# Two layer norms, the linear layer and the set-up of the second attention, split by batch and placed inside the two attentions

## The reference

```python
x = x + _L0_attn_ref(_layernorm(x), ...)  # causal softmax attention, 16 heads of 64, then proj
x = x + _L0_ffn_ref(_layernorm(x), ...)   # base = x @ W.T plus a routed low-rank term, below
x = x + _L1_attn_ref(_layernorm(x), ...)  # softmax of minus squared distances, 16 heads of 8
x = x + _L1_ffn_ref(_layernorm(x), ...)   # shared expert + 2 of 8 experts of width 512
```

## Time and profile before

| | us |
|---|---|
| median of three runs | 1101.64 (1101.56 to 1103.21) |
| the profiled execution, whole | 1099.16 |
| its span, first to last instruction | 1097.4 |
| mean granted TensorE clock in the span | 0.961 |

### The profile page before, as it was taken

How to read it: one execution, slowest core, us unless ns; L and a number is a source line. 1 busy time by engine, 2 the same in 40 slices (tenths; PEclk the granted TensorE clock), 3 DMA queues, 4 the chain that set the end, 5 groups by cost and what they waited for, 6 DMA issues and landing times.

```text
span 1097.4 us, 18772 instructions
## 1 busy us (share of the span) xinstructions
PE 1004.7 (92%) x6927; PEld 596.8 (54%) x6927; DVE 700.0 (64%) x1454; ACT 707.4 (64%) x1031; POOL 556.2 (51%) x482
## 2 busy tenths in 40 slices
PE   4789999999999999999467999999998399999997
PEld 3456666666666666665353222233222277888786
DVE  6777777777777767773463223353122589999998
ACT  3356656666666656665224999999998376666564
POOL 2267877777787778778100000000000157887885
PEclk9899999999999999999768999999999689999999
DMA  2000000000000001100000000000000003121211
GB/s 94 8 9 9 8 9 1 9 8 9 8 9 8 8 8 19 40 1 1 1 1 3 9 12 13 10 9 13 13 8 9 4 1 118 58 94 60 77 39 39
DMA packets 24927, 23.52 MB, mean 21 GB/s; under 512 B 17612, under 2 KB 20316, under 8 KB 23820
## 3 DMA queue, kind: packets, MB, share of 16 engines
q1 hardware_dynamic: 24844, 22.42, 7.2%
HBM read 19.20 MB, written 1.11 MB: 19 GB/s over the span
## 4 chain that ended last, share of the span: by engine, by line
PE 66%; DVE 18%; issue 9%; ACT 3%; SPq 1%; POOL 1%; DMA 1%; DVEq 0%; ACTq 0%; POOLq 0%
PE banks L470 11%; PE banks L1054 10%; PE banks L1042 7%; DVE big L1359 5%; PE banks L338 5%; PE banks L395 4%; PE banks L444 4%; PE banks L478 3%; PE banks L489 3%; PE banks L450 3%; PE banks L448 3%; PE banks L446 3%; PE banks L421 2%; ACT prob L570 2%; PE banks L994 2%
## 5 line engine op out<-in xcount | busy, mean ns | idle before, releaser
L773 POOL TENSOR_TENSOR pacc<-pacc,prob 128x1024 f32<-128x1024 f32 (+3 forms) x160 | 274.7, 1717 | 58.4 <-ACT prob L570 46.8
L1063 ACT ACTIVATE prob<-banks 128x1024 f32<-128x1024 f32 x256 | 238.7, 1099 | 21.4 <-PE banks L1042 21.4
L570 ACT ACTIVATE prob<-banks 128x1024 f32<-128x1024 f32 (+1 forms) x160 | 150.4, 941 | 132.3 <-PE banks L450 128.0
L1392 POOL TENSOR_TENSOR big<-prob,big 128x512 fp32r<-128x512 f32 x108 | 165.1, 1548 | 59.7 <-ACT big L1342 33.0
L470 PE MATMUL banks<-prob,v 128*64 128x512 f32 (+3 forms) x768 | 142.7, 493 | 0.6 <-DVE zz L697 0.3
L1348 ACT ACTIVATE prob<-banks,w 128x512 f32<-128x512 f32 x144 | 94.4, 685 | 71.5 <-PE banks L1310 71.3
L1008 POOL TENSOR_TENSOR wqkv<-wqkv 64x512 f32<-64x512 f32 x8 | 8.3, 1032 | 258.0 <-DVE wqkv L1004 258.0
L1054 PE MATMUL banks<-prob,v 128*32 128x512 f32 x1024 | 137.1, 608 | 0.8 <-DVE pacc L1071 0.3
L1042 PE MATMUL banks<-big 32*128 32x512 f32 x512 | 108.9, 512 | 6.7 <-DVE big L1029 5.8
L1330 PE MATMUL banks<-big 128*128 128x512 f32 x432 | 106.7, 393 | 4.4 <-POOL big L1392 4.4
L1042 PEld LDWEIGHTS banks<-big 32*128 32x128 f32 x512 | 46.1, 185 | 116.5 <-ACT prob L1063 81.0
(11 more groups left out here) (221 smaller groups left out, 1704.5 us busy)
## 6 DMA issues: line engine op xcount, KB each, us to landing
prob<-gate_rows SPq DMA_DIRECT2D x8, 1024.0 KB, 4.7
w<-in_experts SPq DMA_DIRECT2D x9, 514.0 KB, 3.6
wqkv<-in_wqkv SPq DMA_DIRECT2D x16, 193.0 KB, 2.4
x<-in_x SPq DMA_DIRECT2D x4, 256.0 KB, 4.0
zz<-pacc SPq DMA_DIRECT2D x64, 16.0 KB
wpr<-pacc SPq DMA_DIRECT2D x64, 16.0 KB
out<-x SPq DMA_DIRECT2D x4, 256.0 KB, 2.3
wpr<-in_wpr SPq DMA_DIRECT2D x1, 512.0 KB, 6.0
```

What stands on the lines that cost most here:

```text
L570: act.activation(pr[:, g % NRING, :, 0:wd], banks[:, 2 * (j % 2):2 * (j % 2) + 2, 0:wd], ACT.Exp, scale=SCALE0).then_inc(s_exp, 1)
L773: pool.tensor_tensor(pacc[:, half, :, o:BLK], pacc[:, half, :, o:BLK], p_[:, :, at:at + wd], ALU.add).then_inc(s_padd, 1)
L1063: act.activation(prob[:, n % NP1, :], banks[:, 2 * (n % 3):2 * (n % 3) + 2, :].rearrange("p b c -> p (b c)"), ACT.Exp, scale=2 * SCALE1).t ...
L1392: pool.tensor_tensor(act2[1][:, tb % 2, i, :], hid[:, tb % 2, i, :], act2[0][:, tb % 2, i, :], ALU.subtract).then_inc(s_hlP, 1)
```

## The change: what it does

The rows of x of batch 0 are complete half-way through the first attention, so LN1, the linear layer and LN2 are computed for each batch by itself. For batch 0 they are spread over units 9 to 14 of the first attention: rstd and norm in unit 9, transposes in 10, the down projection in 11, the gated transposes in 12, the two linear products in 13, LN2's transposes and the product for the values (`qtm_mid_pe`) in 14. Unit 15 takes the set-up (merged weights, heads, projection, norms of unit 0 of the second attention). For batch 1 they are spread over units 0 to 3 of the second attention, which need batch 0 only. The tail of unit 15 goes into unit 0 of the second attention. Banks 4 and 5 are then still in use, so the first 16 score groups (`EARLY`) alternate over two pairs of banks in place of three. Buffers that overlapped are moved (r1, hi1 and l1 to rows 10 to 15 of `big`, which are free; the order in the `prob` ring is shifted by 4). The small router steps of batch 0 run on GpSimd and DVE, those of batch 1 on DVE. The evictions from PSUM run on ScalarE for batch 0 and on DVE for batch 1. LN statistics of a tile are taken as soon as the tile is complete. The steps at which units 1 to 7 are prepared change too (`SETUP_AT`). LN3 and all that follows stay as they were.

```diff
-        r1 = big[:, 0:2, :]
...
+        r1 = big[:, 10:12, :]
+        hi1 = big[:, 12:14, :]
+        l1 = big[:, 14:16, :]
...
+                elif n == 11:
+                    pe.wait_ge(lb[0]["xT"], 2)
+                elif n == 12:
+                    pe.wait_ge(s_dne, 1)
...
                 mm = pe.matmul(banks[HP[h], 4 + sbk, :], ones[:, :], pacc[:, sbk, h, :], start=True, stop=True)
             mm.then_inc(s_sum, 1)
 
-        def out_pe(pe, u):
+        def out_pe(pe, u, bank):
             pe.wait_ge(s_zz, 2 * u + 2)
-            if u == 2 * PAIRS - 1:
-                pe.wait_ge(s_xacc, u)
-            elif u < 2 * PAIRS - 2:
+            if u < 2 * PAIRS - 2:
                 pe.wait_ge(s_mx, NR * (u + 2) + 7)
+            elif u == 2 * PAIRS - 2:
+                pe.wait_ge(s_rl, 8)
             for i in range(TB):
                 for h in range(2):
-                    mm = pe.matmul(banks[HP[h], 7, 0:D], zz[:, h, i:SEQ // 2:TB], wpr[:, i, :], start=(i == 0), stop=(i == TB - 1))
...
                         qk_pe(pe, n, x_, bn, 2)
                         qk_pe(pe, n, x_, bn, 3)
                     turn_pe(pe, u, 1, 2)
+                    if last:
+                        heads1_pe(pe, 0)
+                        merged_pe(pe)
                     if not first:
...
+                    if u == 10:
+                        turn_mid_pe(pe, 0, 0, 0, 6)
+                        turn_mid_pe(pe, 0, 0, 1, 7)
+                    elif u == 11:
+                        down_mid_pe(pe, 0, 6)
+                    elif u == 12:
+                        gated_mid_pe(pe, 0, 0, 6)
+                        gated_mid_pe(pe, 0, 1, 7)
+                    elif u == 13:
+                        linear_mid_pe(pe, 0, 0, 6)
+                        linear_mid_pe(pe, 0, 1, 7)
+                    elif u == 14:
+                        turn_mid_pe(pe, 1, 0, 0, 6)
+                        turn_mid_pe(pe, 1, 0, 1, 7)
+                    elif last:
+                        for hf in range(2):
+                            proj1_pe(pe, 0, hf, 6 + hf)
+                        for hf in range(2):
+                            norm1_pe(pe, 0, hf, 6 + hf)
                     pv_pe(pe, u, w, 0, first)
                     pv_pe(pe, u, w, 1, first)
...
@@ -555,6 +583,11 @@
                     if n < 2 * PAIRS - 1:
                         qk_pe(pe, n + 1, w, (n + 1) // PAIRS, 0)
                         qk_pe(pe, n + 1, w, (n + 1) // PAIRS, 1)
+                    elif last:
+                        merged_wo_pe(pe)
+                    else:
+                        qtm_mid_pe(pe, 0, 0, 6)
+                        qtm_mid_pe(pe, 0, 1, 7)
...
                     else:
                         logs_act(act, u - 1, 1)
+                    if u == 10:
+                        xT_mid(act, 0, 0, 0, 6)
+                        xT_mid(act, 0, 0, 1, 7)
...
+                    elif u == 14:
+                        qtm_store_mid(act, 0, 0, 6)
+                        qtm_store_mid(act, 0, 1, 7)
+                    elif last:
+                        merged_store_act(act)
 
 
...
+                    elif u == 14:
+                        norm_mid_dve(dve, 1, 0)
+                elif i == 0:
+                    prep1_dve(dve, 0)
+                    merged_mask_dve(dve)
+                    values_ones_dve(dve, 0)
+                    values1_dve(dve, 0)
...
+                    elif last:
+                        sides1_dve(dve, 0, 0, 6)
+                        sides1_dve(dve, 0, 1, 7)
...
+                        xacc_dve(dve, u - 1, 7)
+                        stats_mid_dve(dve, 0, u - 1)
+                    if u == 9:
+                        norm_mid_dve(dve, 0, 0)
+                    elif u == 11:
+                        router_square_dve(dve, 0)
...
+                    router_project(pool, 0)
+                elif u == 11 and j == 9:
+                    router_newton(pool, 0)
+                elif u == 12 and j == 0:
+                    router_shift(pool, 0)
+                elif u == 12 and j == 2:
+                    router_gate(pool, 0)
+                elif u == 14 and j == 0:
+                    newton_mid(pool, 1, 0)
+                elif u == 15 and j == 2:
+                    square1_pool(pool, 0)
                 pool.wait_ge(s_exp, g + 1)
                 if j in MASKED:
...
+        def norm_mid_dve(dve, k, b):
+            dve.wait_ge(lb[k]["newton"], 4 * b + 4)
+            for n in range(b * TB, (b + 1) * TB):
+                dve.tensor_scalar(xn[:, n, :], x[:, n, :], mv[:, n, 0:1], rs[:, 3, n:n + 1], ALU.subtract, ALU.mult).then_inc(lb[k]["norm"], 1)
+
+        def turn_mid_pe(pe, k, b, half, bank):
+            pe.wait_ge(lb[k]["norm"], TB * b + 4 * (half + 1))
+            if b == 0:
+                pe.wait_ge(s_mx, NR * (11, 15)[k] + 3)
+            elif half == 0:
+                if k == 0:
+                    pe.wait_ge(s_rl, 16)
+            else:
+                pe.wait_ge(lb[k]["xT"], 3)
+            for t in range(4):
+                mm = pe.transpose(banks[:, bank, t * P:(t + 1) * P], xn[:, b * TB + 4 * half + t, :], ident)
+            mm.then_inc(lb[k]["turned"], 1)
...
+        def down_mid_pe(pe, b, bank, part=None):
+            pe.wait_ge(lb[0]["xT"], 2 * b + 2)
+            if b == 0:
+                pe.wait_ge(s_mx, NR * 12 + 3)
+            for t in range(TB) if part is None else range(4 * part, 4 * part + 4):
+                c = b * SEQ + t * P
+                mm = pe.matmul(banks[:, bank, t * DALL:(t + 1) * DALL], xT[:, c:c + P], wdn[:, :], start=True, stop=True)
...
+        def router_project(e, b):
...
+            e.tensor_tensor(lw[:, tiles(b), :], dn[b][:, :, DOWN:DALL], across(simn[:, 1, :]), ALU.add).then_inc(s_ch, 1)
+            e.tensor_tensor(pj[b], dn[b][:, :, 0:PROJ], across(small[:, 0:PROJ]), ALU.add).then_inc(s_ch, 1)
+            e.wait_ge(s_ch, c0 + 2)
+            e.tensor_tensor(sq[b], pj[b], pj[b], ALU.mult).then_inc(s_ch, 1)
...
+            for t in part:
+                c = b * SEQ + half * BLK + t * P
+                to = banks[:, bank, t * P:(t + 1) * P]
+                pe.matmul(to, xT[:, c:c + P], wbase[:, :], start=True, stop=False)
+                mm = pe.matmul(to, hgT[b][half][:, t * P:(t + 1) * P], wup[:, :], start=False, stop=True)
...
+        def x_mid_dve(dve, b, half, bank):
+            dve.wait_ge(s_fo, 2 * b + half + 1)
+            xs = x[:, b * TB + 4 * half:b * TB + 4 * half + 4, :].rearrange("p t d -> p (t d)")
+            dve.tensor_tensor(xs, banks[:, bank, :], xs, ALU.add).then_inc(s_fx, 1)
...
+        SETUP_AT = ((2, (4, 9), (5, 10)), (2, (5, 9), (6, 10)), (1, (2, 6), (3, 7)), (4, (5, 9), (6, 10)),
+                    (3, (5, 10), (7, 12)), (3, (5, 10), (7, 12)), (0, (3, 9), (6, 12)))
...
+        def merged_pe(pe):
+            pe.matmul(banks[:, 6, 0:P], wvT[:, :], wkT[:, :], start=True, stop=True).then_inc(s_a1, 1)
...
             if hf == 0:
                 pe.wait_ge(s_qc, u + 1)
-            elif bank == 7:
+                if u == 0:
+                    pe.wait_ge(s_a1m, 1)
+            elif u > 0:
                 pe.wait_ge(s_rl, 8 * u + 4)
...
+        EARLY = 16
+
+        def pair1(n):
+            return n % 2 if n < EARLY else (n - EARLY + 2) % 3
...
-            if n > 2:
-                pe.wait_ge(s_exp1, n - 2)
+            if n < 2:
+                pe.wait_ge(s_exp, 2 * PAIRS * NS - 1 + n)
+            elif n == EARLY:
+                pe.wait_ge(s_xacc, 2 * PAIRS)
+            else:
+                pe.wait_ge(s_exp1, before1(n) + 1)
...
-            act.activation(prob[:, n % NP1, :], banks[:, 2 * (n % 3):2 * (n % 3) + 2, :].rearrange("p b c -> p (b c)"), ACT.Exp,
+            elif prob1(n) < NRING:
+                j = 4 + (prob1(n) - 4) % NRING
+                act.wait_ge(s_pv, NS * (2 * PAIRS - 1) + j + 1)
+                act.wait_ge(s_padd, 12 * (2 * PAIRS - 1) + ADDED[j])
...
+                    if u == 0:
+                        if i == 0:
+                            pv_pe(pe, u0, 1, 8, False)
+                            pv_pe(pe, u0, 1, 9, False)
+                        elif i == 1:
+                            sums_pe(pe, u0, 1)
+                        elif i == 6:
+                            out_pe(pe, u0, 4)
+                        elif i in (13, 14):
+                            turn_mid_pe(pe, 0, 1, i - 13, 7)
+                        elif i == 15:
+                            down_mid_pe(pe, 1, 7, 0)
+                    elif u == 1:
+                        if i == 0:
+                            down_mid_pe(pe, 1, 7, 1)
+                        elif i in (13, 14):
+                            gated_mid_pe(pe, 1, i - 13, 7)
+                    elif u == 2:
+                        if i in (10, 11):
+                            linear_mid_pe(pe, 1, 0, 7, (2 * i - 20, 2 * i - 19))
+                        elif i in (13, 14):
```

(76 more changed lines are left out.)

440 lines of the change are left out of this document (265 added, 175 removed).

## The result

| | us |
|---|---|
| before, median of 4 | 1101.83 (1101.56 to 1103.21) |
| after, median of 4 | 1074.39 (1072.92 to 1076.41) |
| ratio after to before | 0.9742, 95% interval 0.9721 to 0.9764 |
| profiled execution after, whole / span | 1073.41 / 1071.7 |

The change brought 27 us, where 44 were predicted; 1074.4 lies above the range of 1047 to 1071. The page of the changed kernel, to be held against the earlier trace rows: busy shares, the slices of PE and of its clock, the chain.

What follows compares the result with a forecast made beforehand. PE was taken to bound the first attention, a serial chain the seam, ACT to pace the second attention. Terms -64.5 + 13.0 + 7.4 = -44.1 us, from 1101.6, gave a forecast of 1057 us, range 1047 to 1071.

Steps and rivals of the forecast that it cites:

- Term 1: Seam between the two attentions: its chain leaves the path, set-up moves into unit 15; -64.5 us.
- Term 2: Batch 0's work in units 9 to 14: 88 passes at 0.12 us plus 2.5 us of stalls; +13.0 us.
- fourth rival: Waits in the 11 units with new work drop the clock to 0.5; slower than before, 1114 us; chance 0.02.
- Term 3: Second attention, first to last exponential: added work in units 0 to 3, less respacing in 4 to 6; +7.4 us.
- second rival: DVE and POOL block each other on SBUF, operations take 2.4 times as long; +9 us, 1066; chance 0.20.
- (b): Cause named in the experiments, not the prediction: norms on DVE run beside GpSimd's additions.
- (c): Cause named in the experiments, not the prediction: side operations on DVE run beside GpSimd's additions.
- hidden slack: Rival: PE absorbs 5 of 10.5 us of passes, pieces in units 1 to 3 half hidden; 1049 us; chance 0.18.
- row of waits in units 0 to 3: Rival: in-order waits in second attention, 3 to 4 us per unit over the terms; 1071 us; chance 0.07.

Runs made afterwards that it cites:

- out_later: Changed kernel with unit 15's output projection of unit 14 moved behind the value products of slots 4 and 5; 1074.0 us, ratio 0.9738.
- grouped_b0: Changed kernel with batch 0's linear layer in unit 13 running four base passes, then four low-rank passes, per half; 1067.6 us, ratio 0.9667.
- norms_early: Changed kernel with LN2's statistics, aggregation and norms of batch 0 moved forward into unit 13; 1069.9 us, ratio 0.9707.
- grouped_both: Changed kernel with the linear layer's passes grouped by row count for both batches; 1064.6 us, ratio 0.9657.
- combined: Changed kernel with grouped_both, norms_early and out_later together; 1056.9 us, ratio 0.9579.

## Why the prediction was wrong, by its own steps

- **Term 1 (-64.5): nearly right, it measured -61.9.** First exponential after unit 15's start: 31.6 us, 29.0 predicted. Its weak step is "DVE's share (prep, memset, two `sides1_dve`) lies in a unit in which DVE is busy 12 of 34 us": DVE had the time, but the second half of `sides1_dve` met POOL's additions (4.13 for 1.00 us), and `out_pe` stood in the wrong place. With out_later's order 0.9 us of the 2.6 are left.
- **Term 2 (+13.0): this is the step that failed; it measured +25.6.** The count was right: PE has 1608 passes in units 9 to 14, and 1520 before, 88 more. Units 10, 11 and 12, with 8, 16 and 8 of them, grew by 1.2, 2.1 and 1.3 us, and unit 9 by 0.8. What failed is "I use 0.12 for all" in unit 13: the earlier trace rows had 128-row passes back to back and 16-row passes back to back, and the change puts them in turn. Sixteen pairs at 0.41 are 6.6 us, 2.3 more than the 4.34 of grouped_b0; the half clock took the other 4.6 of its 6.9. And "I put 1.5 us there" for unit 14: the hole was 3.49, from norms at 5.23 in place of 2.39 us, and it brought the clock down. The fourth rival had been set aside because "no added wait is worth more than some 2 us". 6.9 us go with norms_early, and 1.6 come back in unit 13. With both cured the term is +13.5.
- **Term 3 (+7.4): right, +8.3.** Unit 0 took 36.4 us as worked out, unit 1 +0.9 (+1.2), unit 3 +2.5 (+2.5), units 4 to 6 together -2.0 (-1.5; 1.6 of it lie in unit 4 alone, so that the respacing gave it is not shown). Unit 2 took +4.1 in place of +2.7: the same mixing, 1.9 us by grouped_both.
- **The second rival** had the mechanism of (b) and (c). Of its places unit 14 was right; unit 9, also given +3, grew by 0.8 in all, though its norms took 3.98 us; and in unit 15 it named the last sums, not the side operations. Its one factor of 2.4 was 2.2 for the norms of unit 14 and 4.1 for the side operations, since what is lost is the rest of an addition and no share of the operation. It was given 0.20 and +9 us, worked out without the clock. The fourth had the clock, but only through holes, and with 0.02. In unit 14 the two met: a hole of 3.5 us priced by its length costs twice that when PE then runs at half clock. In unit 13 neither applied: the passes in turn and the fall of the clock without a hole stood in no rival. That unit took 11.4 us more than before where 3.8 were counted, so it has 7.6 of the 12.6 us by which term 2 was short. The 2.4 us at the start stood in no term either.
- **The other two rivals:** no hidden slack, since 32 passes in units 10 to 12 cost 4.5 us, 0.14 each; no row of waits in units 0 to 3, since their growth of 10.4 us together is near the 8.9 of the term.
- **Luck.** The combined kernel comes out at 1056.9 us, where 1057 was forecast. It is another kernel, and its unit 15, units 9 to 14 and second attention are +0.9, +0.5 and -1.1 us off their terms, with 2.2 us more at the start: that the whole agrees so closely is chance.

## What to carry to other kernels

A stage's price from a trace holds for its order too: look at what stands beside an instruction (row counts on TensorE, GpSimd's additions beside DVE) before the duration is carried to a new place. Work on DVE that reads and writes SBUF, however small (8 columns took 2.32 us), goes where GpSimd is idle, and behind the maxima for which TensorE waits, not in front of them. And a wait of a few us inside a full TensorE stream is to be priced with a second term, the half clock that may follow.

## What the runs showed of the hardware

- A change between 128 and 16 or 64 rows on TensorE costs 0.19 us (pairs start 0.41 apart, runs of four 0.64, runs of eight 1.09), with the low-rank operands and with the base weights' own rows.
- The clock can fall where the profile shows no idle time of PE: with 16-row and 128-row passes in runs of two (six of six executions) or four (one of one), not in runs of eight (none of three), not with 64 rows (one execution). Why is left open.
- A hole of 3.3 to 3.5 us in unit 14 brought the clock down in all nine executions that have it; one of 2.44 to 2.48 us in unit 15 did in four of nine executions.
- The same two DVE operations took 1.00 us beside an idle GpSimd and 4.13 beside its additions, in one execution; one on 8 columns took 0.17 us in one kernel and 2.32 in another. That one, the first norm of unit 9 and the slow pair of unit 15 ended 0.03 to 0.29 us after one of GpSimd's additions.
